# Newton iterations spread over GpSimd's steps, four normalised tiles placed elsewhere on VectorE, and three set-up groups in other PSUM banks

## The reference, cut to what matters

```python
x = x + tanh(g_xattn) * xattn(layernorm(x), ctx, Wq, Wk, Wv, Wo, bo)   # x: 2 x 1024 x 256, ctx: 2 x 64 x 256
x = x + tanh(g_ffn)   * moe(layernorm(x), gate_w, w1, b1, w2, b2)
# xattn: 16 heads of 64; scores over 64 keys, softmax, values, Wo, bias
# moe: router on the mean over the tokens of a batch row, the best 2 of 8 experts for the whole row,
#      each expert gelu(y @ w1 + b1) @ w2 + b2 with 1024 hidden columns
# layernorm(x) = (x - mean) / sqrt(var + 1e-5), no scale and no shift
```

## Time and profile before

| | |
|---|---|
| median of 3 runs | 321.41 us |
| the profiled execution | 321.67 us |
| its span (first to last instruction) | 319.7 us |
| TensorE busy, of the span | 313.2 us, 98% |
| VectorE busy | 236.5 us, 74% |
| ScalarE busy | 164.6 us, 52% |
| GpSimd busy | 84.5 us, 26%, all of it in the first half |
| granted clock of TensorE | 0.9 or more of full speed in every slice |

### The profile page before, as it was taken

How to read it: one execution, slowest core, us unless ns; L and a number is a source line. 1 busy time by engine, 2 the same in 40 slices (tenths; PEclk the granted TensorE clock), 3 DMA queues, 4 the chain that set the end, 5 groups by cost and what they waited for, 6 DMA issues and landing times.

```text
span 319.7 us, 5709 instructions
## 1 busy us (share of the span) xinstructions
PE 313.2 (98%) x1861; PEld 269.9 (84%) x1861; DVE 236.5 (74%) x563; ACT 164.6 (52%) x577; POOL 84.5 (26%) x158
## 2 busy tenths in 40 slices
PE   8999999999999999999999999999999999999996
PEld 7878998878988999888788888888887899888896
DVE  1889999989989999999998475466767554442643
ACT  2648565686766768766366254444543442321320
POOL 1325547586476655425600000000000000000000
PEclk9999999999999999999999999999999999999999
DMA  7997300300000009500016250000020000000012
GB/s 261 386 330 9 35 3 1 133 1 3 0 0 3 0 2 331 195 3 0 2 8 255 79 187 0 0 0 0 24 99 11 2 0 0 2 0 0 2 66 67
DMA packets 21918, 19.99 MB, mean 63 GB/s; under 512 B 11708, under 2 KB 17540, under 8 KB 21508
## 3 DMA queue, kind: packets, MB, share of 16 engines
q1 hardware_dynamic: 21616, 19.14, 19.9%
q10 hardware_dynamic: 276, 0.52, 0.4%
HBM read 17.56 MB, written 2.11 MB: 62 GB/s over the span
## 4 chain that ended last, share of the span: by engine, by line
PE 71%; POOL 10%; DVE 7%; issue 7%; DMA 2%; ACT 2%; SPq 0%; POOLq 0%; DVEq 0%
PE ps L1153 22%; PE ps L1154 22%; PE ps L1155 22%; POOL sx L504 4%; DMA xt<-in_x_dram 2%; POOL xs L524 2%; PE ps L1238 2%; POOL xs L522 2%; ACT sx L636 1%; DVE mx L903 1%; PE ps L1173 1%; DVE pT_lo L862 1%; PE ps L1326 1%; DVE sm L873 1%; PE ps L1424 1%
## 5 line engine op out<-in xcount | busy, mean ns | idle before, releaser
L723 ACT ACTIVATE gel<-ps,b1sel 128x512 f32<-128x512 f32 x64 | 43.9, 690 | 95.5 <-PE ps L1155 95.4
L1112 DVE CAST h_hi<-gel 128x512 fp32r<-128x512 f32 x64 | 28.4, 444 | 58.8 <-ACT gel L723 58.5
L636 ACT ACTIVATE sx<-ps,mx 128x64 f32<-128x64 f32 x128 | 38.3, 325 | 26.2 <-DVE mx L903 26.1
L1153 PE MATMUL ps<-yT_hi,w_hi 128*128 128x512 f32 (+1 forms) x128 | 50.5, 395 | 0.0
L1154 PE MATMUL ps<-yT_lo,w_hi 128*128 128x512 f32 (+1 forms) x128 | 50.0, 390 | 0.0
L1155 PE MATMUL ps<-yT_hi,w_lo 128*128 128x512 f32 (+1 forms) x128 | 49.9, 390 | 0.0
L1114 DVE TENSOR_TENSOR h_lo<-gel,h_hi 128x512 fp32r<-128x512 f32 x64 | 44.9, 702 | 2.2
L504 POOL TENSOR_TENSOR sx<-sx,rs 128x512 f32<-128x512 f32 x32 | 33.5, 1066 | 41.5 <-DVE rs L878 40.8
L1153 PE MATMUL ps<-h_hi,w_hi 128*128 128x512 f32 x96 | 38.4, 400 | 0.0
L1155 PE MATMUL ps<-h_hi,w_lo 128*128 128x512 f32 x96 | 37.5, 390 | 0.0
L1154 PE MATMUL ps<-h_lo,w_hi 128*128 128x512 f32 x96 | 37.4, 390 | 0.0
(11 more groups left out here) (149 smaller groups left out, 670.3 us busy)
## 6 DMA issues: line engine op xcount, KB each, us to landing
stage_w<-in_L_ffn_w_dram SPq DMA_DIRECT2D x7, 1024.0 KB, 7.4
out_dram<-xt SPq DMA_DIRECT2D x6, 256.0 KB, 2.3
wqT<-in_L_xattn_Wq_dram SPq DMA_DIRECT2D x2, 512.0 KB, 7.2
wv_sb<-in_L_xattn_Wv_dram SPq DMA_DIRECT2D x2, 512.0 KB, 8.8
wo_sb<-in_L_xattn_Wo_dram SPq DMA_DIRECT2D x1, 1024.0 KB, 13.9
xt<-in_x_dram SPq DMA_DIRECT2D x1, 1024.0 KB, 10.6
xs<-in_xT_dram SPq DMA_DIRECT2D x1, 1024.0 KB, 11.1
spread<-x_stat SPq DMA_DIRECT2D x1, 1024.0 KB, 4.6
```

Source lines behind the costliest of these rows:

```text
L636: last = nc.scalar.activation(sx[:, par, c0:c0 + M], ps[:, 2 * par + 1, c0 - BANK:c0 - BANK + M], ACT.Exp, bias=mx[:, par, h:h + 1], accum ...
L723: nc.scalar.activation(gel[:, f % 4, :], ps[:, h_bank, :], ACT.Gelu, bias=b1sel[:, b, slot, f:f + 1]).then_inc(gelu_done, 1)
L1112: nc.vector.tensor_copy(h_hi[:, f % 4, :], gel[:, f % 4, :]).then_inc(hhi_ready, 1)
L1153: mm(acc, hi_w, hi_x, start=start, stop=False)
```

## The change

Three edits, and no arithmetic is added or taken away.

1. `GRP_BANK`: the groups ("A", 6), ("A", 7) and ("vT", 0) move from the banks 3, 4, 2 to 2, 3, 4. The pair of A6 and A7 then waits for the reads of kT1 and A0, no longer of A0 and A1. On VectorE the first `a_lo` goes ahead of the copy of `tg`.
2. `newton` is split: `newton_head` (the wait for the guess and the first product) and `newton(..., times)`. For x, tiles 8 to 15, two iterations stay at the end of step 4 and the third comes in step 5 behind the product with `rs`. For y, tiles 0 to 3 and 4 to 7, the head and one iteration stand at the head of steps 6 and 10, and two iterations at the end of the same steps, so nothing is left at the head of steps 7 and 11. Step 15 stays as it was.
3. `y_tile` of tile 0 moves in VectorE's step 7 ahead of the two late `vw` groups. `y_tile` of tiles 1, 2 and 3 moves from the end of steps 8, 9 and 10 to between the statistics and `pT_lo` of the same steps 8, 9 and 10.

```diff
-        GRP_BANK = dict(zip(groups, [0, 1, 2, 3, 4, 5, 6, 0, 1, 3, 4, 2, 6, 4, 5, 0, 6] + [0, 1] * len(LATE)))
+        GRP_BANK = dict(zip(groups, [0, 1, 2, 3, 4, 5, 6, 0, 1, 2, 3, 4, 6, 4, 5, 0, 6] + [0, 1] * len(LATE)))
...
+        Y_FIRST, Y_WHILE = 7, {8: 1, 9: 2, 10: 3}
...
-                if s in (7, 11, 15):
-                    y_rstds((s - 7) // 4)
+                if s in (6, 10):
+                    y_head((s - 6) // 4)
+                    newton(*Y_PARTS[(s - 6) // 4], rstd2, 1)
+                if s == 15:
+                    y_head(2)
+                    y_rstds(2, 3)
...
+                if s == 5:
+                    newton(*X_PARTS[2], rstd1, 1)
+                    pool.sem_inc(x_rstd, 1)
                 if active(s + LEAD) and s + LEAD >= XT0:
                     x_scaled(s + LEAD)
+                if s in (6, 10):
+                    y_rstds((s - 6) // 4, 2)
...
                 if s == 4:
-                    newton(*X_PARTS[2], rstd1, ve_x, 3)
-                    pool.sem_inc(x_rstd, 1)
+                    newton_head(*X_PARTS[2], ve_x, 3)
+                    newton(*X_PARTS[2], rstd1, 2)
...
             x_norm(0)
+            group(*A0[0])
             dve.wait_ge(tg_spread, 1)
             nc.vector.tensor_copy(tg[:, :], ps[:, 7, 0:2]).then_inc(tg_ready, 1)
-            for g in A0[:6]:
+            for g in A0[1:6]:
                 group(*g)
...
+                if s in Y_WHILE:
+                    y_tile(Y_WHILE[s])
...
+                if s == Y_FIRST:
+                    y_tile(0)
                 if s in LATE:
...
-                    if y is not None:
+                    if y is not None and y > 3:
                         y_tile(y)
```

More of the change, by code:

```diff
@@ L462, in link, with newton_head, newton @@
                 pool.wait_ge(pool_step, pn[0])
-            def newton(t0, t1, rstd, var, guess):
+            def newton_head(t0, t1, var, guess):
+                pool.wait_ge(guess_ready, guess)
+                link(nc.gpsimd.tensor_scalar(ve_p[:, 0:t1 - t0], var[:, t0:t1], -0.5, None, ALU.mult))
+            def newton(t0, t1, rstd, times):
                 r, n = rstd[:, t0:t1], t1 - t0
@@ L468, in newton @@
                 tt, ts = nc.gpsimd.tensor_tensor, nc.gpsimd.tensor_scalar
-                pool.wait_ge(guess_ready, guess)
-                link(ts(v, var[:, t0:t1], -0.5, None, ALU.mult))
-                for _ in range(3):
+                for _ in range(times):
                     link(tt(u, v, r, ALU.mult))
@@ L476, in newton, with y_head, y_rstds @@
                     link(tt(r, u, r, ALU.mult))
-            def y_rstds(i):
-                newton(*Y_PARTS[i], rstd2, ve_y, len(X_PARTS) + i + 1)
+            def y_head(i):
+                newton_head(*Y_PARTS[i], ve_y, len(X_PARTS) + i + 1)
+            def y_rstds(i, times):
+                newton(*Y_PARTS[i], rstd2, times)
                 pool.sem_inc(y_rstd, 1)
             def step(s, par):
-                if s in (7, 11, 15):
-                    y_rstds((s - 7) // 4)
+                if s in (6, 10):
[4 more added lines that the diff above has]
+                    y_rstds(2, 3)
                 t = s + LEAD
@@ L505, in step @@
                                                 ALU.mult).then_inc(mul_done, 1)
+                if s == 5:
+                    newton(*X_PARTS[2], rstd1, 1)
+                    pool.sem_inc(x_rstd, 1)
                 if active(s + LEAD) and s + LEAD >= XT0:
                     x_scaled(s + LEAD)
+                if s in (6, 10):
+                    y_rstds((s - 6) // 4, 2)
                 if s == 1:
[L509 removed]
+                    newton_head(*X_PARTS[1], ve_x, 2)
+                    newton(*X_PARTS[1], rstd1, 3)
                     pool.sem_inc(x_rstd, 1)
                 if s == 4:
[L512 to L513 removed]
+                    newton_head(*X_PARTS[2], ve_x, 3)
+                    newton(*X_PARTS[2], rstd1, 2)
             def x_scaled(t):
```

## The result

| | before | changed |
|---|---|---|
| median, same chip | 321.51 us (22 runs, 321.14 to 321.82) | 321.89 us (22 runs, 321.67 to 322.26) |
| ratio | | 1.0014, interval 1.0009 to 1.0020 |
| span of the profiled execution | 319.7 us | 319.9 us |

The forecast was 0.5 us faster (320.9), with a range up to 321.7. The kernel became 0.4 us slower: 321.89 lies outside the range, and the interval excludes no change. (The kernel before measured 321.51 here, 0.10 above the 321.41 from which the forecast was counted.) That is the side of rival D, and D's mechanism: tiles of y moved forward lengthen the circle of VectorE and ScalarE.

The account below looks back on a forecast made before the run. The prediction took a circle of VectorE and ScalarE, nearly as long as TensorE's step, to bound the kernel: 0.4 from the set-up plus 0.1 from cheaper tiles of y gives 0.5 faster, 320.9 us, range 319.9 to 321.7.

Parts of the forecast that it names:

- rival D: Slower: three tiles of y moved ahead of pT_lo lengthen the circle, 0.9 each in steps 8 and 10; 322.1 us, chance 0.08.
- the circle of VectorE and ScalarE: Steps 5 to 15: maxima, heads, pT_hi, pT_lo, reciprocal, next maxima; 6.94 us a turn, TensorE running ahead only by its slack.
- Part 1, 0.4: Set-up: banks and first a_lo let everything behind, the circle too, start 0.4 us earlier; bounds 0 and 0.62.
- Part 2 for x, 0: Steps 4 and 5: TensorE's stall in step 6 goes but comes back one step later; worth 0, bound 0.7 us.
- Part 2 for y: Steps 6, 7, 10, 11: products no longer wait for Newton iterations; 0.52 us off TensorE in step 11, nothing in step 7.
- Part 3, "I take 0": Moved tiles of y: about even for the circle, taken as 0; bounds +0.9 and -0.5 us.
- Step 8 gets 0.33 added: Tile 1 of y ahead of step 8's pT_lo falls into GpSimd's idle time and adds 0.33 us.
- Tile 0 falls at the seam of two GpSimd instructions, 0.45 instead of 1.02: Tile 0 of y, moved ahead of the late vw groups, costs VectorE 0.45 us instead of 1.02.
- The bound of +0.9: Worst case of the moved tiles of y for the circle: both tiles at 0.9 us.
- I add 0.1 for tiles of y that cost VectorE less: Circle a further 0.1 us earlier, since tiles of y cost VectorE less than before.
- The signs: Right if tile 0's maxima at 19.5, reciprocals of steps 6 and 11 at 60.5 and 95.7, new step 7 wait 0.4 to 0.9.
- C: Nothing gained: the tile in step 8 costs what the set-up edit gives; 321.4 us, chance 0.14.

Follow-up runs that it names:

- g1: Kernel before plus three bn_stats on VectorE in step 7, written to a tile nothing reads: 321.41 us against 321.65, ratio 0.9994.
- g2: Kernel before plus the same three unused bn_stats on VectorE, in step 13: 322.26 us, ratio 1.0021.
- e1: Kernel before with only the bank moves and the first a_lo ahead of tg: 321.31 us against 321.64, ratio 0.9985.
- e2: Kernel before with only the Newton iterations split over the steps, for x and y: 321.54 us against 321.64, ratio 0.9997.
- f5: e4 with VectorE's late vw groups moved ahead of the subtraction sx, guess for y kept in step 6: 321.22 us against 321.65, ratio 0.9987.
- e4: Changed kernel without the moved tiles of y, so banks, first a_lo and Newton split only: 321.24 us against 321.64, ratio 0.9990.
- e3: Kernel before with only the tiles of y moved, tile 0 ahead of vw, tiles 1 to 3 ahead of pT_lo: 322.10 us against 321.64, ratio 1.0015.
- f2: e4 with tiles 1 to 3 of y moved ahead of pT_lo, tile 0 left behind the vw groups: 321.85 us, ratio 1.0001 against the kernel before.
- g3: Kernel before with banks, first a_lo and late vw groups ahead of sx, no Newton iteration moved: 320.54 us against 321.65, ratio 0.9968.
- f4: f3 with the late vw groups ahead of the subtraction sx and out_bias ahead of the maxima: 321.15 us against 321.77, ratio 0.9983.
- f3: e4 with VectorE's guess for y and its Newton iterations moved from step 6 to step 7: 321.59 us against 321.77, ratio 0.9989.

## Why the prediction was wrong

- **The circle.** Right. g1 and g2 show it, and at step 16 circle and TensorE met as said: TensorE's transposes are 0.28 later (126.80), the reciprocal 0.25 (130.63 against 130.38).
- **Part 1, 0.4.** Right in kind. From the key products to the first maxima the five traces without part 1 show 9.69 to 9.94, the nine with it 9.25 to 9.59; their means lie 0.44 apart. In the medians it is 0.33 (e1).
- **Part 2 for x, 0.** Right in size as far as e2 shows it, whose interval reaches from -0.45 to +0.23 and which moves the iterations for x and y together; wrong in place. TensorE's wait didn't come back "one step later" on the product, but in the same step: 0.72 for VectorE's late `vw` groups, which the stall on the product had covered. With those moved as well (f5) it stood as 0.9 for `pT_lo`. So TensorE waited in step 6 for three different things in turn, and from e4 to f5, where one of these waits went and the next came, the circle stayed the same.
- **Part 2 for y.** The products start on time, as forecast. What the sum left out is that `x_scaled`, which stands behind the product on GpSimd, starts as much earlier: at 69.60 in step 7, where it was 71.15. Part 3 puts tile 0 at just that point: 1.18, where the same new place without part 2 cost 0.52 (e3), and the old place with part 2 cost 0.80 (e4).
- **Part 3, "I take 0". This is the step that failed.** "Step 8 gets 0.33 added" was right (0.31, f2). "Tile 0 falls at the seam of two GpSimd instructions, 0.45 instead of 1.02" was wrong: 1.18. So the circle had lost 0.55 at step 8 against before, and not 0: 0.31 for tile 1 (from the residual to `pT_lo` 1.10 instead of 0.79), 0.16 for tile 0 (from `sx` to the residual 3.02 instead of 2.86), and 0.08 that was there in step 6 already. Step 10 lost another 0.2, which the sum had left out though rival D named it. The bound of +0.9 held, the middle didn't. The prediction itself said that tile 0 "could as well come to 1.0: then the circle would lose 0.5 at step 8", and that happened. It should have had a chance of its own, not a place in a sentence. The prediction took it from the Trainium skill (SBUF — State Buffer, Who interferes with whom), by which the second to ask is blocked for the whole instruction. The trace agrees that tile 0 waits for the GpSimd instruction that it met: it ends 0.15 behind it. That is less than the 0.40 that a tile takes with GpSimd idle (72.71), so the trace doesn't show that nothing of the tile ran before.
- **"I add 0.1 for tiles of y that cost VectorE less."** They do (625 ns in the median instead of 882), but the circle didn't get it. Tile 2, for one, went from 0.84 to 0.49, but now stands ahead of a `pT_lo` for which VectorE sat idle another 0.64 all the same.
- **Rival D** had the right mechanism at too small a chance (0.08). Its size, 0.9 for each tile in steps 8 and 10, was too large: the moved tiles 1 and 3 took 0.40 and 0.41. "It decides as soon as the circle's loss at step 8 is above part 1's gain" held: 0.55, against 0.33 in the medians.
- **The signs.** Tile 0's maxima at 19.5 and the reciprocal of step 6 at 60.5 came (19.50, 60.60). The reciprocal of step 11 did not (96.42, forecast 95.7), nor did the new wait on the product in step 7. `pT_lo` of step 8 at 73.02 was the sign for C and D; the tiles above 0.8 that were to go with it did not come, except for tile 0.

As a sum of medians and circles: part 1 -0.33 (median of e1), part 2 -0.23 (circle of e2), part 3 +0.87 (circle against e4) give +0.3; measured +0.38.

Why f2's circle loses only 0.19 in step 10, with a tile of 0.41 more ahead of `pT_lo`, can be read from its rows against those of e4: tile 2 (0.84) no longer stands at the end of step 9, so the residual of step 10 comes 0.38 sooner behind the reciprocal; the first instruction of the guess meets `x_scaled` and costs 0.17 more from start to start; tile 3, with the 0.22 that it waits for the guess, adds 0.41.

Open: why 0.94 in the circle of g2 is 0.61 in the median, and at what distance between two starts the order of VectorE and GpSimd turns over.

## What to carry to other kernels

- A table of waits names who is waited for, not what sets the period. Where two engines form a closed circle of the same length as the busy engine's step, look in each step for the instruction of the circle that doesn't wait: only work ahead of that one counts (g1 against g2: 0.04 less and 0.94 more in the circle).
- When a stall is taken away on one engine, follow everything behind it, above all work that shares something with the engine that sets the period. Moving Newton iterations saved TensorE 0.3 a time and cost VectorE about 0.4 a time (f5 against g3); leaving them and moving only `vw` and part 1 gave 1.1 us (g3), where part 1 alone gave 0.3 (e1).
- Where an instruction falls near the border of another engine's, its price has two values. Give both a chance; don't take the lower.

## What the runs showed of the hardware

- The price of a VectorE instruction beside GpSimd is decided by where it starts. The same 128x256 tile of y took 0.40 (GpSimd idle, 72.71 in the changed kernel), 0.52 (e3), 0.80 (e4) and 1.18 (changed kernel). Each of the dear ones ended 0.15 behind a GpSimd instruction: 70.69 against 70.54 in the changed kernel, 71.88 against 71.73 in f5. In the 14 traces there are 49 tiles of y of 0.49 and more that stand alone in their row; all of them end 0.14 to 0.16 behind the end of a GpSimd instruction. So the price is what that instruction still has to run, and 0.15.
- Where the tile starts just before one GpSimd instruction ends and the next begins, one of two prices comes up. Ahead of the next one by 0.02 (before) and 0.09 (changed kernel), the tile had to wait for the whole next instruction; ahead by 0.14 (g3) it did not. Nothing in between was measured. The 0.33 of the earlier trace rows is of this kind as well: GpSimd was idle only when that tile started at 32.03, and its next product began at 32.19.
- Small instructions pay too: 128x4 took 0.15 to 0.17 alone and 0.62 (f5), 0.82 (f4), 0.83 (f3), each time ending with GpSimd's instruction (57.89 against 57.86; 63.71 against 63.68; 64.90 against 64.88).
- Not every instruction pays: the three added `bn_stats` took 1.08 in g1 (63.53 to 64.61) as in g2, though in g1 GpSimd's `x_scaled` ran beside them (two instructions, 63.17 to 65.03) and in g2 GpSimd was idle (its last instruction ended at 107.35).
